# A vision-tower kernel on one core: one filter block's five-shift sum goes from VectorE to GpSimd, and two convolution products change places

## Chip, cores and metric

One core of one Trainium2 chip runs the whole program in one launch. The metric is the device time in microseconds (us); lower is better. All data is float32.

## What is computed

The reference takes 64 images of 84x84x3 and the weights of three blocks, and returns 64 x 25 tokens of 128 values:

```
xs = concat([x, shift_right(x), shift_left(x), shift_down(x), shift_up(x)])   # 15 channels
y  = conv2d(xs, conv_w, strides=(16, 16), "VALID") + conv_b                   # 25 tokens per image
y  = (y - mean(y)) * rsqrt(var(y) + 1e-3) * gamma + beta
h  = y @ dense_w + dense_b
h  = layernorm(h + attention(h))      # two softmax maps, their difference weighted by lambda, group norm
h  = layernorm(h + ffn(h))            # per-image FFN weights: W + sum over 8 experts of gate * tv_W
```

Only the first block, the tokenizer, is touched by the change. A shift of the image and a shift of the filter are the same thing, so the convolution over 15 channels can be done as one over the 3 image channels, with one filter that is the sum of the five shifted ones. The host lays out the five shifted copies of the filter (`conv_filter`, each on an 18x18x3 window, 972 rows of 128, padded to 1024, with the bias as one more row). The kernel sums them.

## The kernel before

**Tokenizer.** The 1024 rows of the filter are cut into KT = 8 blocks of 128 rows, which this text counts as k = 0 to 7; k = 6 is the seventh. The 1600 tokens are cut into steps of 256 for the loads and into units u = 0 to 3 for the work: three units of 512 tokens (two steps each) and one of 64. For each k:

- SyncE (`load_filter`, L398) loads the five copies of block k, 128 x 640 values, 320 KB, and adds 16 to `w_loaded[k]`.
- VectorE (`weff_sum(k)`) waits for that load, sums the five copies in one TENSOR_REDUCE (L787) into `wsum[:, k]`, waits for its own result, and sums each row of that to one number with a second TENSOR_REDUCE (L789, `rowsum`).
- ScalarE (`weff_centre(k)`, L560) waits for the row sum and writes rowsum - 128 * wsum, the centred filter block `weff[:, k]`, so that the layer norm's mean is zero without further work.
- TensorE (`conv(u, k)`, L1078) multiplies `weff[:, k]` with unit u's windows of block k, and adds over k into one PSUM bank for each unit. Each call stands in the trace as two weight loads and two MATMULs. Before an even k it waits for the windows of blocks k and k+1 of both steps (`load_windows`, L403: index j = k/2 and step s), and always for `weff_ready >= k + 1`.

VectorE runs `weff_sum(0)` to `weff_sum(7)` one after another as its first work, then `y_scale(0)`. ScalarE runs `weff_centre(0)` to `weff_centre(7)`, then `h_bias()` (L579), `y_square(0)` (L564), `y_rstd(0)` (L568, L570). All engines run in their written order, and a wait holds all that is behind it on that engine.

SyncE issues the loads in this order: filter 0; windows j=0, s=0,1; filter 1; windows j=0, s=2,3; filters 2, 3; windows j=1, s=0,1; filters 4, 5; windows j=2, s=0,1; filters 6, 7; windows j=3, s=0,1; the first constants (L418); windows of s=2,3 for j=1, 2, 3; the second constants (L421); windows of the last three steps; the last constants (L424).

**Order on TensorE.** It is written out by hand, from L1249 on. The part that matters:

```
conv(0, 0)  conv(1, 0)  conv(0, 1)  conv(1, 1)  conv(0, 2)  conv(0, 3)  conv(0, 4)  conv(0, 5)  conv(0, 6)
conv(1, 2)
conv(0, 7)
h_bias_product()          # L1084, 128x1; releases h_bias() on ScalarE
conv(1, 3)
y_var(0)                  # L1093, needs y_square(0)
conv(1, 4)  conv(1, 5)  conv(1, 6)  dense(0)  conv(1, 7)  proj(0, 0) ...
```

`conv(0, 7)` ends the sum of the first 512 tokens, and `y_square(0)` reads it. `conv(1, 2)` needs the windows j=1 of steps 2 and 3.

**GpSimd** begins with small memsets (L464 to L474), then waits for the first constants and makes `dgam` (L476, L478: gamma times the dense weights, needed by `dense(0)`), then for the second constants, makes small tiles from them (L482 to L491), clears `wrow` (L493, four memsets) and goes on with copies and softmax products. In the trace its first additions (TENSOR_TENSOR) come at L476.

**Later stages.** Projections (L1128), attention scores (L1172), value products (L1187), group norm, output projection, the gates, the merging of the per-image FFN weights (L1387, evacuated by VectorE at L382 and ScalarE at L381), their application (L1409, L1433), and the last two layer norms. `keep_long` (L1246) are products whose result nobody reads.

Of the kernel before, what the change touches and what calls it, by code (L numbers as in the profile page):

```python
# [29 lines left out]
KT = 8  # L30
NP = KT // 2
NSH = 5
# [55 lines left out]
UT = 2 * ST  # L88
Y_BANK = [2, 3, 2, 3]
VAR_BANK = 7  # L90
PROJ_BANK = [4, 5, 6, 4]
SLOT = [0, 0, 0, 0, 1, 0, 1, 0]


def unit_tokens(u):

    return min(UT, NTOK - u * UT)


def unit_steps(u):  # L100

    return range(2 * u, min(2 * u + 2, NSTEP))
# [10 lines left out]
def build(nc, cst_d, wconv_d, xcol_d, tvw_d, sce_d, scb_d, out_d):  # L113
    f32 = mybir.dt.float32
    bf16 = mybir.dt.bfloat16
    ALU = mybir.AluOpType
    ACT = mybir.ActivationFunctionType
    AX = mybir.AxisListType
    ctx = ExitStack()
    with ctx:  # L120
# [3 lines left out]
        def sem(name):  # L124
            return ctx.enter_context(nc.semaphore(name))
# [16 lines left out]
        def C(name, rows=P):  # L142
            a, b = COL[name]
            return cst[0:rows, a:b]
# [5 lines left out]
        w5 = hid[:, 0:KT * NSH * D]  # L150
        weff = hid[:, KT * NSH * D:KT * (NSH + 1) * D].rearrange("p (k d) -> p k d", k=KT)
        wsum = t6[:, 0:KT * D].rearrange("p (k d) -> p k d", k=KT)
        rowsum = sb("rowsum", KT)

        def windows(u, k):

            n = unit_tokens(u)
            a = arena[:, KT * UT * u:KT * UT * u + KT * n]
            if n < UT:
                return a.rearrange("p (k n) -> p k n", k=KT)[:, k]  # L160
            return a.rearrange("p (s k n) -> p s k n", s=2, k=KT)[:, :, k, :]

        def unit_cols(t, u):

            return t[:, UT * u:UT * u + unit_tokens(u)]
# [65 lines left out]
        w_loaded = [sem(f"w_loaded{i}") for i in range(KT)]  # L231
# [7 lines left out]
        rows_loaded = sem("rows_loaded")  # L239
        stored = sem("stored")  # L240
        wsum_done = sem("wsum_done")
        rowsum_done = sem("rowsum_done")
        weff_ready = sem("weff_ready")
        conv_done = sem("conv_done")
# [218 lines left out]
        def _(pool):  # L463
# [8 lines left out]
            for b in range(2):  # L472
                pool.memset(qT[b][:, NTOK:TP], 0.0).then_inc(pads_set, 1)
            pool.memset(t1[:, NTOK:].rearrange("p (b k) -> p b k", k=IB)[:, :, NS:IB], 0.0).then_inc(pads_set, 1)  # L474
            pool.wait_ge(first_loaded, 16)
            pool.tensor_tensor(dgam[:, :], C("dense_w"), C("gamma").to_broadcast([P, P]), ALU.mult).then_inc(dgam_ready, 1)  # L476
            pool.wait_ge(dgam_ready, 1)
# [65 lines left out]
            for s in range(NPS):  # L543
                pool.wait_ge(norm_done[2], 2 * (s + 1))
                c = slice(s * ST, (s + 1) * ST)
                v = t4[:, c].rearrange("p (t d) -> p t d", d=D)
# [6 lines left out]
        def _(act):  # L553
# [12 lines left out]
            def y_rstd(u):  # L566
                act.wait_ge(yvar_done, u + 1)
                act.activation(unit_cols(t5, u), PS[:, VAR_BANK, 0:unit_tokens(u)], ACT.Ln, bias=epsc[:, 0:1]).then_inc(yln_done, 1)  # L568
                act.wait_ge(yln_done, u + 1)
# [6 lines left out]
            def h_bias():  # L576
                act.wait_ge(first_loaded, 16)
                act.wait_ge(hb_done, 1)
                act.activation(hb[:, :], PS[:, VAR_BANK, 0:1], ACT.Identity, bias=C("dense_b")).then_inc(hb_ready, 1)  # L579

# [4 lines left out]
            def query_evac(c):  # L585
                act.wait_ge(proj_done[0], c + 1)
                act.activation(qT[0][:, c * QT:(c + 1) * QT], PS[:, PROJ_BANK[0], 0:QT], ACT.Copy).then_inc(proj_ready[0], 1)

            def keys_evac(c, b):
# [3 lines left out]
                act.wait_ge(proj_done[w], c + 1)  # L593
                src = PS[:, PROJ_BANK[w], 0:QT].rearrange("p (u k) -> p u k", u=2)
                for m in range(4):
# [185 lines left out]
        def _(dve):  # L781

            def weff_sum(k):

                dve.wait_ge(w_loaded[k], 16)
                v = w5.rearrange("p (k g d) -> p k d g", k=KT, g=NSH)[:, k]
                dve.tensor_reduce(wsum[:, k, :], v, AX.X, ALU.add).then_inc(wsum_done, 1)  # L787
                dve.wait_ge(wsum_done, k + 1)
                dve.tensor_reduce(rowsum[:, k:k + 1], wsum[:, k, :], AX.X, ALU.add).then_inc(rowsum_done, 1)  # L789

            def y_scale(u):
# [23 lines left out]
            def small_evac():  # L815
                dve.wait_ge(small_done, 1)
                dve.tensor_copy(cob[:, :], PS[:, VAR_BANK, 0:1]).then_inc(cob_ready, 1)
                dve.tensor_copy(lnaff[:, :], PS[:, VAR_BANK, 128:128 + 2 * D]).then_inc(lnaff_ready, 1)

            def key_evac(c):  # L820
                dve.wait_ge(kb_ready, 2)
                dve.wait_ge(proj_done[1], c + 1)
                src = PS[:, PROJ_BANK[1], 0:QT].rearrange("p (u k) -> p u k", u=2)
                for m in range(4):
# [3 lines left out]
            def key_raw():  # L828

                dve.wait_ge(second_loaded, 16)  # L830
                dve.wait_ge(proj_done[1], 2)
                src = PS[:, PROJ_BANK[1], 0:QT].rearrange("p (u k) -> p u k", u=2)
                dve.tensor_scalar(k1raw, src, C("k1_b"), None, ALU.add).then_inc(k1raw_ready, 1)

            def query_evac(b, c):
                w = 2 * b
                dve.wait_ge(proj_done[w], c + 1)
                dve.tensor_copy(qT[b][:, c * QT:(c + 1) * QT], PS[:, PROJ_BANK[w], 0:QT]).then_inc(proj_ready[w], 1)

# [73 lines left out]
            def gate_sum(q):  # L913
                dve.wait_ge(gh_ready, q + 1)
                dve.tensor_reduce(ghsum[:, q * QI:(q + 1) * QI], by_image(t5, q), AX.X, ALU.add).then_inc(ghsum_done, 1)

            weff_sum(0)
            weff_sum(1)
            weff_sum(2)
            weff_sum(3)  # L920
            weff_sum(4)
# [143 lines left out]
        def _(pe):  # L1065
            def conv(u, k):

                n = unit_tokens(u)
                if k % 2 == 0:
                    for s in unit_steps(u):  # L1070
                        pe.wait_ge(x_loaded[k // 2][s], 16)
                pe.wait_ge(weff_ready, k + 1)
                if k == 0 and u >= 2:
                    pe.wait_ge(h_ready, u - 1)
                dst = PS[:, Y_BANK[u], 0:n]
                if n == UT:
                    dst = dst.rearrange("p (s n) -> p s n", s=2)
                mm = pe.matmul(dst, weff[:, k, :], windows(u, k), start=(k == 0), stop=(k == KT - 1))  # L1078
                if k == KT - 1:
                    mm.then_inc(conv_done, 1)  # L1080

            def h_bias_product():
                pe.wait_ge(first_loaded, 16)
                pe.matmul(PS[:, VAR_BANK, 0:1], C("dense_w"), C("beta"), start=True, stop=True).then_inc(hb_done, 1)  # L1084

            def y_var(u):
# [4 lines left out]
                else:  # L1091
                    pe.wait_ge(yln_done, u)
                pe.matmul(PS[:, VAR_BANK, 0:unit_tokens(u)], yavg[:, :], unit_cols(t5, u), start=True, stop=True).then_inc(yvar_done, 1)  # L1093

# [19 lines left out]
            def proj(c, w):  # L1114
# [11 lines left out]
                if w == 3:  # L1126
                    pe.wait_ge(proj_ready[0], c + 1)
                pe.matmul(PS[:, PROJ_BANK[w], 0:QT], C(("q1", "k1", "q2", "k2")[w]), t2[:, c * QT:(c + 1) * QT], start=True, stop=True).then_inc(proj_done[w], 1)  # L1128

# [124 lines left out]
            conv(0, 4)  # L1254
            conv(0, 5)
            conv(0, 6)
            conv(1, 2)
            conv(0, 7)
            h_bias_product()
            conv(1, 3)  # L1260
            y_var(0)
# [318 lines left out]
```

## Time and profile before

| | us |
|---|---|
| median of 3 runs | 214.38 |
| lowest and highest of them | 212.93, 216.39 |
| the profiled execution | 213.37 |
| its span, first to last instruction | 211.6 |
| granted TensorE clock, mean over the span | 0.956 of full |

The profiled execution is a run of its own beside the three. Its span leaves out 213.37 - 211.6 = 1.8 us that lie around the instructions. Engines in the rows: PE is TensorE's matmuls, PEld its weight loads, DVE is VectorE, ACT ScalarE, POOL GpSimd, SPq the issue of a DMA by SyncE. Times of rows are counted from the span's start.

### The profile page before, as it was taken

The numbers are of one execution on the slowest core, as the hardware profiler recorded it, in microseconds if no ns is written. First come the engines' busy times: TensorE is split into PE (matmuls) and PEld (weight loads), VectorE is DVE, ScalarE is ACT, GpSimd is POOL, SyncE is SP. The second block draws the span as 40 slices with busy tenths as digits, with TensorE's granted clock in tenths as the row PEclk, the third lists the DMA queues.
The fourth block names the chain that finished last, engine by engine and source line by source line (L and its number), as shares of the span: only waits on it lengthen the run. The fifth ranks groups of instructions, "written<-read, shape, count | busy, mean of one in ns | idle before, by whom it ended". The sixth has DMA issues, their size and how long they took to land.

```text
span 211.6 us, 7823 instructions
## 1 busy us (share of the span) xinstructions
PE 176.7 (84%) x3432; PEld 121.3 (57%) x3432; DVE 134.4 (64%) x247; ACT 120.6 (57%) x223; POOL 55.5 (26%) x80
## 2 busy tenths in 40 slices
PE   0797999999999999898899999999999999980000
PEld 0233444466668765544788888888877777760000
DVE  2594146466999899784596666666664444489750
ACT  2131365387794523588475777777763333356991
POOL 2001681584278546000000000000070000037740
PEclk9999999999999999999999999999999999997555
DMA  6999994222200000000013121213000000000112
GB/s 203 384 392 386 375 300 110 83 84 64 59 6 3 5 3 3 6 0 0 3 31 86 55 64 46 71 37 81 5 5 3 3 3 3 3 3 0 39 47 69
DMA packets 9265, 16.51 MB, mean 78 GB/s; under 512 B 1598, under 2 KB 4350, under 8 KB 8720
## 3 DMA queue, kind: packets, MB, share of 16 engines
q1 hardware_dynamic: 9232, 16.02, 23.8%
q8 instruction: 27, 0.44, 0.9%
q14 instruction: 6, 0.05, 0.1%
HBM read 15.20 MB, written 0.82 MB: 76 GB/s over the span
## 4 chain that ended last, share of the span: by engine, by line
PE 62%; DVE 14%; ACT 11%; SPq 4%; DMA 4%; issue 3%; ACTq 0%
PE PS L1387 16%; DVE arena L382 8%; PE PS L1078 8%; PE PS L1409 7%; PE PS L1128 5%; ACT t L769 5%; PE PS L1246 4%; PE PS L1399 4%; PE PS L1172 4%; DMA arena<-windows 4%; PE PS L1187 3%; SPq L403 2%; PE PS L1146 2%; SPq L398 2%; PE PS L1098 2%
## 5 line engine op out<-in xcount | busy, mean ns | idle before, releaser
L382 DVE COPY arena<-PS 128x1024 f32<-128x1024 f32 x32 | 39.0, 1224 | 32.4 <-PE PS L1387 32.4
L381 ACT ACTIVATE arena<-PS 128x1024 f32<-128x1024 f32 x32 | 32.7, 1024 | 21.0 <-PE PS L1387 20.9
L1387 PE MATMUL PS<-gates,wrow 32*128 32x128 f32 x1024 | 37.2, 282 | 1.7 <-DVE arena L382 0.7
L1387 PEld LDWEIGHTS PS<-gates,wrow 32*128 32x128 f32 x1024 | 31.4, 186 | 7.8 <-DVE arena L382 5.3
L1078 PE MATMUL PS<-arena,hid 128*128 128x512 f32 (+1 forms) x64 | 27.3, 564 | 7.7 <-ACT hid L560 6.2
L1078 PEld LDWEIGHTS PS<-arena,hid 128*128 128x128 f32 x64 | 11.4, 205 | 21.7 <-issue 15.7
L539 POOL TENSOR_TENSOR t<-t,lnaff 128x2048 f32<-128x2048 f32 x1 | 4.6, 4568 | 71.2 <-PE PS L1399 71.2
L1433 PE MATMUL PS<-arena,hid 128*32 128x128 f32 x512 | 17.3, 276 | 0.0
L1409 PE MATMUL PS<-arena,t 128*32 128x128 f32 x512 | 17.3, 276 | 0.0
L769 ACT ACTIVATE t<-t,nms,rsl 128x128 f32<-128x128 f32 x32 | 13.4, 480 | 2.4 <-DVE nms L1048 2.4
L734 ACT ACTIVATE hid<-hid 128x400 f32<-128x400 f32 x16 | 8.5, 537 | 10.7 <-DVE hid L1005 10.7
L1433 PEld LDWEIGHTS PS<-arena,hid 128*32 128x32 f32 x512 | 13.0, 109 | 2.7 <-issue 2.7
L547 POOL TENSOR_TENSOR t<-t,lnaff 128x256 f32<-128x256 f32 x8 | 5.8, 726 | 32.6 <-ACT t L769 32.6
L1409 PEld LDWEIGHTS PS<-arena,t 128*32 128x32 f32 x512 | 13.0, 109 | 1.9
L787 DVE TENSOR_REDUCE t<-hid 128x128 f32<-128x640 f32 x8 | 9.9, 1244 | 6.1 <-DMA hid<-conv_filter 6.1
L1128 PE MATMUL PS<-t,cst 128*128 128x400 f32 x32 | 12.6, 512 | 0.3 <-ACT hid L596 0.3
L521 POOL TENSOR_TENSOR arena<-arena,wr 128x800 f32<-128x800 f32 x8 | 12.3, 1538 | 0.6
L560 ACT ACTIVATE hid<-t,rowsum 128x128 f32<-128x128 f32 x8 | 3.2, 402 | 13.5 <-DVE rowsum L789 13.5
L1399 PE MATMUL PS<-cst,t 128*128 128x128 f32 x64 | 10.5, 286 | 0.4 <-ACT t L727 0.4
L596 ACT ACTIVATE hid<-PS,kb,headmask 128x400 f32<-128x400 f32 x16 | 9.7, 688 | 0.5 <-PE PS L1128 0.3
L1246 PE MATMUL PS<-t,cst 128*128 128x512 f32 x20 | 9.9, 608 | 0.0
L727 ACT ACTIVATE t<-PS 128x512 f32<-128x512 f32 x16 | 9.3, 581 | 1.0 <-PE PS L1409 1.0
(133 smaller groups left out, 302.5 us busy)
## 6 DMA issues: line engine op xcount, KB each, us to landing
arena<-windows SPq DMA_DIRECT2D x24, 256.0 KB, 8.2
wrow<-ffn_weights SPq DMA_DIRECT2D x32, 128.0 KB
hid<-conv_filter SPq DMA_DIRECT2D x8, 320.0 KB, 6.3
wrow<-ffn_weights SPq DMA_DIRECT2D x64, 8.0 KB
cst<-consts SPq DMA_DIRECT2D x1, 840.0 KB, 11.6
out<-t SPq DMA_DIRECT2D x16, 50.0 KB
cst<-consts SPq DMA_DIRECT2D x1, 322.0 KB, 9.3
arena<-windows SPq DMA_DIRECT2D x4, 64.0 KB, 8.7
```

What stands on the lines that cost most here:

```text
L381: return eng.activation(dst, PS[:, b:b + 2, :], ACT.Copy)
L382: return eng.tensor_copy(dst, PS[:, b:b + 2, :])
L521: pool.tensor_tensor(ev, ev, wr[:, c].unsqueeze(2).to_broadcast([P, UX, NS]), ALU.mult).then_inc(scaled, 1)
L769: act.activation(dst[:, c], t4[:, c], ACT.Identity, bias=nms[:, k:k + 1], scale=rsl[:, k:k + 1]).then_inc(norm_done[L], 1)
L787: dve.tensor_reduce(wsum[:, k, :], v, AX.X, ALU.add).then_inc(wsum_done, 1)
L1078: mm = pe.matmul(dst, weff[:, k, :], windows(u, k), start=(k == 0), stop=(k == KT - 1))
L1128: pe.matmul(PS[:, PROJ_BANK[w], 0:QT], C(("q1", "k1", "q2", "k2")[w]), t2[:, c * QT:(c + 1) * QT], start=True, stop=True).then_inc(proj_do ...
L1246: pe.matmul(PS[:, bank, :], ident, t2[:, 0:512], start=True, stop=True)
L1387: mm = pe.matmul(PS[:, merge_bank(n) + r, :].rearrange("p (b k j) -> p k b j", k=4, j=NJ)[:, k], wrow[32 * r:32 * r + 32, w], gates[32 * r ...
L1399: mm = pe.transpose(PS[:, 6 + i % 2, g * P:(g + 1) * P], t1[:, c:c + P], ident)
L1409: mm = pe.matmul(PS[32 * (b % 4):32 * (b % 4) + 32, 4 + i % 2, (b // 4) * P:(b // 4 + 1) * P], t3[:, im * IB:(im + 1) * IB], wm[c % 2][:, ...
L1433: mm = pe.matmul(PS[32 * (b % 4):32 * (b % 4) + 32, 4 + q, (b // 4) * D:(b // 4 + 1) * D], hidv[:, c, im * NS:im * NS + 32], wm[c % 2][:, ...
```

## The change

Two edits. GpSimd, ahead of its wait for the first constants, waits for filter block KG = 6 and makes its five-shift sum by four additions, each of which waits for the one before; VectorE's `weff_sum(6)` no longer does the first TENSOR_REDUCE but waits for the fourth addition, and then makes the row sum as before. And on TensorE `conv(0, 7)` stands ahead of `conv(1, 2)` instead of behind it.

```
+KG = 6
...
+        wpart_done = sem("wpart_done")
...
             pool.memset(t1[:, NTOK:].rearrange("p (b k) -> p b k", k=IB)[:, :, NS:IB], 0.0).then_inc(pads_set, 1)
+            v = w5.rearrange("p (k g d) -> p k g d", k=KT, g=NSH)[:, KG]
+            pool.wait_ge(w_loaded[KG], 16)
+            pool.tensor_tensor(wsum[:, KG, :], v[:, 0], v[:, 1], ALU.add).then_inc(wpart_done, 1)
+            for g in range(2, NSH):
+                pool.wait_ge(wpart_done, g - 1)
+                pool.tensor_tensor(wsum[:, KG, :], wsum[:, KG, :], v[:, g], ALU.add).then_inc(wpart_done, 1)
             pool.wait_ge(first_loaded, 16)
...
             def weff_sum(k):
-                dve.wait_ge(w_loaded[k], 16)
-                v = w5.rearrange("p (k g d) -> p k d g", k=KT, g=NSH)[:, k]
-                dve.tensor_reduce(wsum[:, k, :], v, AX.X, ALU.add).then_inc(wsum_done, 1)
-                dve.wait_ge(wsum_done, k + 1)
+                if k == KG:
+                    dve.wait_ge(wpart_done, NSH - 1)
+                else:
+                    dve.wait_ge(w_loaded[k], 16)
+                    v = w5.rearrange("p (k g d) -> p k d g", k=KT, g=NSH)[:, k]
+                    dve.tensor_reduce(wsum[:, k, :], v, AX.X, ALU.add).then_inc(wsum_done, 1)
+                    dve.wait_ge(wsum_done, k + 1 if k < KG else k)
                 dve.tensor_reduce(rowsum[:, k:k + 1], wsum[:, k, :], AX.X, ALU.add).then_inc(rowsum_done, 1)
...
             conv(0, 6)
+            conv(0, 7)
             conv(1, 2)
-            conv(0, 7)
             h_bias_product()
```

## Rows read from the trace of the kernel before

**Rows 1.** The page: busy us of each engine, share of the span, instructions.

```profile
PE 176.7 (84%) x3432; PEld 121.3 (57%) x3432; DVE 134.4 (64%) x247; ACT 120.6 (57%) x223; POOL 55.5 (26%) x80
```

**Rows 2.** The chain that ended last, 0 to 80 us: start, us, what.

```profile
9.49 8.02 DMA arena<-windows
...
19.13 1.95 PE PS L1078 x4
...
52.75 2.42 ACT hid L596 x4
```

**Rows 3.** Timeline, TensorE's weight loads: start, us; in brackets idle before, and releaser.

```profile
17.57 0.30 PEld L1078 LDWEIGHTS PS<-arena,hid 128*128 128x128 f32 x2 [1.45 <-DMA arena<-windows]
19.10 0.30 PEld L1078 LDWEIGHTS PS<-arena,hid 128*128 128x128 f32 x2 [1.23 <-DMA arena<-windows]
...
22.10 0.30 PEld L1093 LDWEIGHTS PS<-t,yavg 128*128 128x128 f32 x2 [0.77 <-ACT t L564]
```

**Rows 4.** Timeline of VectorE, 15 to 17 us.

```profile
15.05 0.29 DVE L789 TENSOR_REDUCE rowsum<-t 128x1 f32<-128x128 f32 x1
15.28 1.25 DVE L787 TENSOR_REDUCE t<-hid 128x128 f32<-128x640 f32 x1
16.56 0.29 DVE L789 TENSOR_REDUCE rowsum<-t 128x1 f32<-128x128 f32 x1
16.77 1.24 DVE L787 TENSOR_REDUCE t<-hid 128x128 f32<-128x640 f32 x1
```

**Rows 5.** Timeline of ScalarE, 16 to 22 us.

```profile
16.88 0.40 ACT L560 ACTIVATE hid<-t,rowsum 128x128 f32<-128x128 f32 x1 [1.11 <-DVE rowsum L789]
18.36 0.40 ACT L560 ACTIVATE hid<-t,rowsum 128x128 f32<-128x128 f32 x1 [1.07 <-DVE rowsum L789]
21.30 0.26 ACT L579 ACTIVATE hb<-PS,cst 128x1 f32<-128x1 f32 x1 [2.54 <-PE PS L1084]
21.46 0.59 ACT L564 ACTIVATE t<-PS 128x512 f32<-128x512 f32 x1
```

**Rows 6.** Loads of filter blocks 6 and 7, issued at 7.92 and 8.52 us.

```profile
L398 SPq DMA_DIRECT2D hid<-conv_filter x2: 434/493/552, 7.9 to 8.5; - x2
DMA to landing us min/median/max: 7.3/7.5/7.6
```

**Rows 7.** Window loads j=1 of steps 2 and 3, issued at 10.44 and 10.87.

```profile
DMA to landing us min/median/max: 7.9/8.0/8.1
```

**Rows 8.** GpSimd's groups by shape: count, busy us, mean ns, idle before.

```profile
L547 POOL TENSOR_TENSOR t<-t,lnaff 128x256 f32<-128x256 f32 x8 | 5.8, 726 | 32.6 <-ACT t L769 32.6
L539 POOL TENSOR_TENSOR t<-t,lnaff 128x2048 f32<-128x2048 f32 x1 | 4.6, 4568 | 71.2 <-PE PS L1399 71.2
L518 POOL TENSOR_TENSOR wr<-rec,lamw 128x32 f32<-128x32 f32 x8 | 2.0, 252 | 14.0 <-DVE rec L863 13.9
L476 POOL TENSOR_TENSOR dgam<-cst 128x128 f32<-128x128 f32 x1 | 0.4, 399 | 15.9 <-DMA cst<-consts 15.9
```

**Rows 9.** Timeline of GpSimd, 2 to 23 us.

```profile
17.77 0.40 POOL L476 TENSOR_TENSOR dgam<-cst 128x128 f32<-128x128 f32 x1 [15.89 <-DMA cst<-consts]
18.26 0.55 POOL L478 TENSOR_SCALAR dgam<-dgam 128x128 f32<-128x128 f32 x1
22.64 0.20 POOL L482 TENSOR_TENSOR rowhalf<-cst 128x2 f32<-128x2 f32 x1 [3.84 <-DMA cst<-consts]
```

**Rows 10.** Stretches: us, busy time of each engine, granted clock (PEclk), DMA share, GB/s.

```profile
12.05:19.00 6.95, 5.82 (x13) 1.88 (x11) 6.14 (x9) 2.01 (x5) 0.95 (x2) 1.00 1.05 386
188.00:193.00 5.00, 1.60 (x42) 1.10 (x34) 4.15 (x21) 3.29 (x11) 3.85 (x6) 0.99 0.00 0
```

**Rows 11.** Timeline: TensorE's weight loads around 12 us, and its last products.

```profile
11.20 0.34 PEld L1078 LDWEIGHTS PS<-arena,hid 128*128 128x128 f32 x1 [0.52 <-issue]
12.05 0.19 PEld L1078 LDWEIGHTS PS<-arena,hid 128*128 128x128 f32 x1 [0.52 <-issue]
12.48 0.19 PEld L1078 LDWEIGHTS PS<-arena,hid 128*128 128x128 f32 x1 [0.24 <-issue]
...
188.52 1.08 PE L1433 MATMUL PS<-arena,hid 128*32 128x128 f32 x32
```

## Prediction, made before the changed kernel ran

> **What bounds the kernel.** I read four views, in this order. The page first: TensorE is busy for 176.7 of 211.6 us, far more than any other engine [rows 1]. Then the chain that ended last, cut to the stretch around the change. It runs over window loads until 17.51 us, then over TensorE; from 19.13 us it is TensorE's own work, piece after piece, until ScalarE takes over for one step at 52.75 [rows 2]. So what moves the moment at which TensorE sets off at 19.13 should move everything behind it by as much. Third, the timeline of each engine between 13 and 25 us, to see who releases whom. Fourth, the GpSimd rows that resemble the new additions.
>
> The timelines give this order of events before. Filter block 6 is issued at 7.92 and lands 7.3 later [rows 6], at 15.2; VectorE starts to sum it at 15.28, 0.06 before the previous row sum is over [rows 4], so the load and VectorE are ready together. The sum takes 1.25, the row sum starts at 16.56, block 7 follows at 16.77 [rows 4]. ScalarE centres block 6 from 16.88 to 17.28 and block 7 from 18.36 to 18.76 [rows 5]. TensorE does conv(0, 6) at 17.57, released not by the filter (ready at 17.28) but by the windows that land at 9.49 + 8.02 = 17.51 [rows 2, 3]. Then conv(1, 2) at 19.10, released by its windows, issued at 10.87 and landed 8.1 later, at about 19.0 [rows 3, 7]. The pair conv(1, 2), conv(0, 7) takes 1.95, to 21.08 [rows 2], and released by the bias product behind it ScalarE does the bias at 21.30 and the square at 21.46 [rows 5].
>
> **The change, part by part.**
>
> *Removed:* one TENSOR_REDUCE of 1.25 us on VectorE. In the written order that alone would bring block 7 forward by up to 1.25, to 17.51.
>
> *Added:* four additions of 128x128 on GpSimd. They need block 6 in full, so they can't start before about 15.28, the moment at which VectorE started on it. GpSimd is idle then: its memsets are done and its next work starts at 17.77 [rows 9]. Duration of one: the nearest row is the 128x128 product with a broadcast operand, 0.399 [rows 8]; between the 128x32 (0.252) and the 128x256 (0.726) a straight line gives 0.252 + 96/224 x 0.474 = 0.455 [rows 8]. I take 0.43, between the two. The step between dependent instructions is 0.09 (18.17 to 18.26) [rows 9]. So 4 x 0.43 + 3 x 0.09 = 1.99, and the sum is ready at 17.27. That is 0.7 later than VectorE had it (16.53). Bounds: with 0.252 each 1.28, ready at 16.56; with 0.726 each 3.17, ready at 18.45.
>
> The Trainium skill, GPSIMD Engine Reference, section Engine selection, gives reductions along the free dimension to VectorE; its section on elementwise accounting has about 2.6 cycles per element and 4497 ns for 2048 columns. The trace agrees with the long case: 4.57 us for 128x2048 [rows 8]. An estimate from that page's figures for 128 columns is 128 x 2.6 / 1.2 GHz = 0.28 plus 0.06 of fixed cost, 0.34, which gives a sum at 16.91 and would leave the total within 0.1 us of before; the 128x128 row here is 0.399, so the row decides.
>
> *The wait that is added:* VectorE's row sum 6 now waits for GpSimd, and queued behind it is the sum of block 7, whose filter landed about 0.9 after block 6 (8.52 + 7.6 = 16.1) [rows 6]. VectorE runs in written order, so it idles from 15.34. Row sum 6 starts at 17.31 instead of 16.56 (0.04 for the release). ScalarE follows 0.32 later (16.56 to 16.88) and takes 0.40: block 6 is ready at 18.03. Conv(0, 6) goes from 17.57 to 18.07; the filter is now what comes last, not the windows. Sum 7 starts 0.21 after row sum 6 (16.56 to 16.77), at 17.52, and block 7 is ready 1.99 after that (16.77 to 18.76): 19.51, against 18.76 before [rows 4, 5].
>
> *The exchange on TensorE:* conv(0, 7) now stands first. It starts at 19.51 + 0.04 = 19.55 in place of conv(1, 2) at 19.10. Conv(1, 2) has had its windows since 19.0 but is queued behind. With the old order conv(1, 2) would still start at 19.10, end its issue 0.86 later at 19.96, and conv(0, 7) would find its filter ready since 19.51: the late block would cost nothing. So the exchange uncovers what GpSimd added. Alone, without GpSimd's part, it would gain: conv(0, 7) at 18.80, the pair over 0.3 earlier. Together the pair starts 19.55 - 19.10 = 0.45 later.
>
> *Behind it:* the bias product comes after both in either order, and ScalarE's square waits behind the bias, so the square of the first tokens doesn't profit from an earlier conv(0, 7); it comes 0.45 later as well. The product that needs it waits for it already (22.10, released by L564) [rows 3]. Everything on the chain follows by 0.45.
>
> *On GpSimd:* the additions are over at 17.27, before the first constants let dgam start at 17.77, so dgam isn't moved; if they took 0.726 each it would start 0.65 late, and its reader, dense(0), needs y_scale(0), which comes behind the square at 21.46 [rows 5]. What follows waits for the second constants at 22.64 anyway [rows 9]. SyncE's queue is untouched. The added instructions cost nothing beyond this.
>
> **Sum.** 213.37 + 0.45 = 213.8 us, against the profiled execution. That execution lies 1.0 below the median of the three runs shown; by the median the same sum gives 214.8. I forecast 213.8, slightly slower, a difference below what can be told (2%, 4.3 us, is about what a measurement of this kernel can tell from no change). With the additions from 0.38 to 0.50 each it is +0.2 to +0.7 us.
>
> **Rivals.**
>
> 1. *It works as drawn: a gain.* If the sum of block 6 is there by 16.56, VectorE loses nothing. With the sum then, block 7 comes at 18.76 as before, the exchange starts the pair at 18.80 instead of 19.10: -0.3, 213.1. If it were there at 15.3, as if the sum were free, block 7 would be ready at 17.5, conv(0, 7) would follow conv(0, 6) directly at 18.46, and the gain would be 0.65: 212.7. For it: VectorE is busy nearly all the time from 10.7 on, and in an execution in which filter 6 lands 0.7 earlier GpSimd would work beside VectorE's sum of block 5. Against it: here the load lands as VectorE gets free, so nothing is left to overlap; and four additions at the price of a 128x32 one are needed.
>
> 2. *The additions are dearer.* At 0.726 each the sum is ready at 18.45, block 7 at 18.49 + 0.21 + 1.99 = 20.69, and the pair starts 1.6 late: 215.0. It decides from 0.5 us each. For it: they are the first additions that GpSimd does, and a plain operand costs more than a broadcast one may. Against it: the 0.399 of L476 is itself a first addition.
>
> 3. *TensorE's clock falls (slower).* The hole before conv(0, 6) grows by 0.50 and the one behind it stays. If the granted clock went from 2.4 to 1.2 GHz there, products would be spaced 0.85 instead of 0.43 us per record (11.20 to 12.05 against 12.05 to 12.48) [rows 11]. An estimate: at that spacing the four records of the pair take 4 x 0.42 = 1.7 us more, the ten from conv(0, 6) to y_var(0) 4.2. With the 0.45 that is 215.5 if the clock is back after the pair, and 218.0 if it isn't before y_var(0) is done, 4.6 over the profiled run and past the limit of 2%. Decided by whether the holes of 1.1 and 0.5 us are enough. Against it: over 12.05 to 19.00 the clock is 1.00 with 5.82 of 6.95 busy, and at the end TensorE is idle from 189.6, and the mean clock of 188 to 193 is still 0.99 [rows 10, 11]. The Trainium skill, TensorE: Matmul & The Clock Gate, section What's actually happening, says that the clock falls back when TensorE has been idle for a while; the trace's end agrees, and its longest new hole is much shorter than those 3.4 us.
>
> 4. *It is drowned.* The change shows nowhere, because a later wait takes up 0.4 us: 213.4. For it: the chain leaves TensorE at 52.75 and crosses VectorE and ScalarE many times later. Against it: those all wait for products of the same chain, and no load with a fixed time ends late on it.
>
> **Chances.** Forecast (+0.2 to +0.7) 0.58; rival 1 0.15; rival 2 0.17; rival 3 0.03; rival 4 0.07. The range must hold the scatter of runs, 212.93 to 216.39, as a median dampens it: 212.6 to 215.8. From below it covers a gain of 0.7, from above the costliest additions and a median like the one shown. Over 2% faster has no case that reaches it: 0.01. Over 2% slower needs the clock: 0.02. Within 2%: 0.97.
>
> **What would show each step.** In the profile after: four TENSOR_TENSOR rows of 0.40 to 0.46 on GpSimd from about 15.28 on, the last over near 17.3; VectorE idle from 15.34 to 17.3, released by GpSimd; ScalarE's seventh and eighth L560 at about 17.6 and 19.1; conv(0, 6) released by ScalarE at 18.0 rather than by a DMA; conv(0, 7) released by ScalarE near 19.5; the bias at 21.7 instead of 21.30; granted clock 1.00 over 12 to 26 us. The forecast is wrong if conv(0, 7) starts before 19.1, if the additions last over 0.5 each, or if the shift of 0.4 at 21 us is not there any more at 50 and at 180 us.

## The result, and the profile after

The changed kernel took 214.23 us (median of 20 runs, 213.17 to 216.29), the kernel before 213.24 in 20 runs of its own (212.46 to 216.39). The ratio is 1.0050, 95% interval 1.0032 to 1.0069: slower by some 1.1 us, within 2% as forecast, but more than twice the forecast 0.45. The ratios leave out single executions that lie over 1.5% above the fastest of their kernel. The direction came out as forecast, and so did the path on which the delay travels; its size did not. The time of 213.8 was forecast from a profiled execution; the measured median lies 0.4 above it, inside the stated range. In the profiled executions the span went from 211.6 to 212.4.

The chain that ended last, in the changed kernel (start, us, what):

```profile
7.78 7.75 DMA hid<-conv_filter
15.52 0.07 issue
15.59 0.47 POOL t L479
...
17.19 0.46 POOL t L482
17.66 0.02 issue
17.68 0.28 DVE rowsum L800
17.96 1.17 DVE t L798
...
19.16 0.30 DVE rowsum L800
19.45 0.02 issue
19.48 0.41 ACT hid L568
19.89 0.04 issue
19.93 1.98 PE PS L1089 x4
21.92 0.12 PE PS L1095 x2
...
53.58 2.42 ACT hid L604 x4
```

Line numbers moved by 2 to 11: L1089 is conv (L1078 before), L568 the centring (L560), L800 and L798 VectorE's two reductions (L789, L787), L604 was L596 and L1444 was L1433. Before, the chain came to TensorE by a load of windows [rows 2]. Now it comes by the load of filter block 6, GpSimd's four additions, the row sum, the sum of block 7 that was queued behind it, its row sum and ScalarE; the conv(0, 7) that sets off at 19.93 is the first of the pair, as this text calls conv(0, 7) and conv(1, 2) together. From there on nothing changed: from the pair's start to ScalarE's step at 53.58 are 33.65 us, and 52.75 - 19.10 = 33.65 before [rows 2, 3]. The shift of 0.83 us is still there in the last products of the feed-forward part, in the chains of the kernel before and of the changed one:

```profile
184.18 1.05 PE PS L1433 x32
185.01 1.05 PE PS L1444 x32
```

The three engines, from their timelines; first GpSimd:

```profile
15.59 0.46 POOL L479 TENSOR_TENSOR t<-hid 128x128 f32<-128x128 f32 x1 [13.71 <-DMA hid<-conv_filter]
16.13 1.52 POOL L482 TENSOR_TENSOR t<-t,hid 128x128 f32<-128x128 f32 x3
18.02 0.40 POOL L484 TENSOR_TENSOR dgam<-cst 128x128 f32<-128x128 f32 x1 [0.37 <-DMA cst<-consts]
```

VectorE (compare [rows 4]):

```profile
15.28 0.28 DVE L800 TENSOR_REDUCE rowsum<-t 128x1 f32<-128x128 f32 x1
17.68 0.28 DVE L800 TENSOR_REDUCE rowsum<-t 128x1 f32<-128x128 f32 x1 [2.12 <-POOL t L482]
17.88 1.24 DVE L798 TENSOR_REDUCE t<-hid 128x128 f32<-128x640 f32 x1
```

TensorE's weight loads (compare [rows 3]):

```profile
16.05 0.30 PEld L1089 LDWEIGHTS PS<-arena,hid 128*128 128x128 f32 x2 [1.00 <-ACT hid L568]
18.51 0.30 PEld L1089 LDWEIGHTS PS<-arena,hid 128*128 128x128 f32 x2 [2.17 <-issue]
19.93 0.30 PEld L1089 LDWEIGHTS PS<-arena,hid 128*128 128x128 f32 x2 [1.12 <-ACT hid L568]
```

VectorE, idle for 2.12 us although block 7 had landed at 16.34, is the added wait; the pair at 19.93, released by ScalarE and not by windows, is the exchange. All loads of this execution landed a little late: filter block 6 at 15.52 against 15.26. The edit's own cost is therefore read from the landing of block 6 on: 3.84 us to the pair before (19.10 - 15.26), 4.41 after (19.93 - 15.52). That is +0.57 us. The rest of the 0.83 between the two pair starts is the loads' own scatter. This way of counting is sound because the loads keep their distances: block 6 landed anywhere from 14.88 to 15.74 in the 14 traces of this text, but block 7 always landed 0.82 to 0.85 behind it, and the windows that release the pair in the kernel before 3.76 to 3.80 behind it. So the 3.84 of the one trace of the kernel before is not a chance of that trace. The distance from landing to pair is what the experiments are compared by below.

### The profile page after: what moved, and what is told of

It reads as the page before. It is cut to its first block, busy times and chain, and to the rows that moved or that the text cites. A ratio compares the mean times of both kernels' runs of the same rounds, so it can differ in the third digit from the quotient of the medians.

```text
span 212.4 us, 7826 instructions
## 1 busy us (share of the span) xinstructions
PE 176.2 (83%) x3432; PEld 121.1 (57%) x3432; DVE 133.3 (63%) x246; ACT 120.6 (57%) x223; POOL 57.3 (27%) x84
## 4 chain that ended last, share of the span: by engine, by line
PE 61%; DVE 14%; ACT 11%; DMA 4%; SPq 3%; issue 3%; POOL 1%; ACTq 0%
PE PS L1398 16%; DVE arena L384 8%; PE PS L1420 7%; PE PS L1089 7%; PE PS L1139 5%; ACT t L777 5%; PE PS L1257 4%; PE PS L1410 4%; PE PS L1183 4%; DMA hid<-conv_filter 4%; PE PS L1198 3%; PE PS L1157 2%; SPq L405 2%; PE PS L1109 2%; PE PS L1104 1%
## 5 line engine op out<-in xcount | busy, mean ns | idle before, releaser
L1089 PE MATMUL PS<-arena,hid 128*128 128x512 f32 (+1 forms) x64 | 26.8, 554 | 9.0 <-DMA arena<-windows 7.1
L1089 PEld LDWEIGHTS PS<-arena,hid 128*128 128x128 f32 x64 | 11.1, 202 | 22.8 <-issue 16.3
L1444 PE MATMUL PS<-arena,hid 128*32 128x128 f32 x512 | 17.3, 276 | 0.0
L1444 PEld LDWEIGHTS PS<-arena,hid 128*32 128x32 f32 x512 | 13.0, 110 | 2.7 <-issue 2.7
L798 DVE TENSOR_REDUCE t<-hid 128x128 f32<-128x640 f32 x7 | 8.7, 1243 | 6.3 <-DMA hid<-conv_filter 6.3
L568 ACT ACTIVATE hid<-t,rowsum 128x128 f32<-128x128 f32 x8 | 3.2, 402 | 14.6 <-DVE rowsum L800 14.6
L604 ACT ACTIVATE hid<-PS,kb,headmask 128x400 f32<-128x400 f32 x16 | 9.7, 688 | 0.4 <-PE PS L1139 0.3
```

The source lines that it names most:

```text
L604: act.activation(keys(b, c)[:, :, m, :], src, ACT.Identity, bias=kb[:, 4 * b + m:4 * b + m + 1], scale=headmask[:, m:m + 1]).then_inc(proj ...
L1444: mm = pe.matmul(PS[32 * (b % 4):32 * (b % 4) + 32, 4 + q, (b // 4) * D:(b // 4 + 1) * D], hidv[:, c, im * NS:im * NS + 32], wm[c % 2][:, ...
```

## The experiments

Theory 1: the pair starts when block 7's filter is ready, that is a fixed time after block 6 lands, and everything behind moves by as much. Rivals: GpSimd's part costs by itself (theory 2), by contention, by VectorE's wait, or by a hole that takes TensorE's clock; or a late pair costs more than its lateness (theory 3). "Landing to pair" is from the trace of each run; "to ScalarE" is from the pair to the step that stands at 52.75 in [rows 2]. With block 7 first the pair follows conv(0, 6) without a gap, and its start is taken as 0.86 behind that of conv(0, 6); the sum of the two distances doesn't depend on that. The first ratio of the changed kernel, 1.0050, is in the section above; each group was measured against its own runs of the kernel before (medians 212.85, 213.02, 213.20), on two chips.

| kernel | landing to pair | to ScalarE | ratio | 95% interval |
|---|---|---|---|---|
| before | 3.84 | 33.65 | 1 | |
| changed, again | 4.41 | 33.65 | 1.0053 | 1.0024 to 1.0083 |
| exchange alone | 3.56 | 33.65 | 0.9978 | 0.9950 to 1.0007 |
| GpSimd alone | 3.82 | 33.68 | 1.0005 | 0.9978 to 1.0033 |
| block 7 first | 3.87 | 33.64 | 1.0015 | 0.9987 to 1.0042 |
| hole filled | 4.42 | 33.65 | 1.0042 | 1.0014 to 1.0070 |
| block 5 | 3.70 | 33.65 | 0.9998 | 0.9973 to 1.0023 |
| square first | 3.56 | 33.45 | 0.9988 | 0.9967 to 1.0010 |
| sum twice | 6.53 | 35.69 | 1.0244 | 1.0207 to 1.0280 |
| twice, filled | 6.55 | 33.65 | 1.0109 | 1.0069 to 1.0148 |

The intervals reach some 0.3% to either side, as much as most of the effects. By the ratios alone the changed kernel differs from the one before, from the exchange alone, from block 5 and from the square first, and the sum done twice differs from all others; what else is said of single rows rests on the traces.

**The exchange alone.** VectorE sums all blocks.

```
             conv(0, 6)
+            conv(0, 7)
             conv(1, 2)
-            conv(0, 7)
             h_bias_product()
```

> The kernel before with the exchange on TensorE alone; VectorE sums all eight blocks. Theory 1 (the pair conv(0, 7), conv(1, 2) starts when block 7 is ready, and all behind it moves by as much): block 7 ready at 18.76, conv(0, 7) at 18.80 in place of a pair start at 19.10, -0.3 us, ratio 0.9985, and the pair's start moves with VectorE's sum, not with the windows. Theory 2 (the exchange itself costs, because conv(1, 2) no longer fills the hole and TensorE's clock suffers in some executions): a wider spread of times, ratio 1.002 or more, some executions with a lower granted clock.

The pair came 0.28 earlier, as expected, released by ScalarE. Weight loads on TensorE:

```profile
17.22 0.30 PEld L1078 LDWEIGHTS PS<-arena,hid 128*128 128x128 f32 x2 [1.44 <-DMA arena<-windows]
18.48 0.30 PEld L1078 LDWEIGHTS PS<-arena,hid 128*128 128x128 f32 x2 [0.95 <-ACT hid L560]
```

and on ScalarE:

```profile
18.02 0.40 ACT L560 ACTIVATE hid<-t,rowsum 128x128 f32<-128x128 f32 x1 [1.07 <-DVE rowsum L789]
```

The chain of this trace names a load of windows as the pair's releaser. The times speak for ScalarE: the pair starts 0.46 after ScalarE's last centring did, as in the changed kernel (19.48 to 19.93), and the windows that conv(1, 2) needs landed only at 18.68, 0.20 after conv(0, 7) had started.

The ratio of 0.9978 agrees with 0.9985 and excludes the 1.002 of theory 2; that it is a gain can't be told from the ratio (its interval holds 1), only from the trace.

**GpSimd's part alone.** The changed kernel with the old order.

```
             conv(0, 6)
-            conv(0, 7)
             conv(1, 2)
+            conv(0, 7)
             h_bias_product()
```

> The changed kernel with the old order on TensorE: conv(1, 2) ahead of conv(0, 7), GpSimd sums block 6. Theory 1: GpSimd's sum makes block 7 ready about 0.8 to 0.9 later than before, near 19.6 for a landing of block 6 at 15.26; conv(1, 2) starts with its windows at 19.10, conv(0, 7) at 19.96 and finds its filter: 0.0 to +0.1 us, ratio 1.000. Theory 2 (GpSimd's part costs by itself, for instance by the longer hole ahead of conv(0, 6)): ratio 1.003 or more.

```profile
18.38 0.30 PEld L1089 LDWEIGHTS PS<-arena,hid 128*128 128x128 f32 x2 [2.14 <-issue]
19.21 0.33 PEld L1089 LDWEIGHTS PS<-arena,hid 128*128 128x128 f32 x2 [0.53 <-issue]
19.80 0.19 PEld L1089 LDWEIGHTS PS<-arena,hid 128*128 128x128 f32 x1 [0.26 <-ACT hid L568]
```

In these weight loads conv(0, 6) is late (18.38, 2.99 after the landing at 15.39, against 2.31 before), conv(1, 2) follows at 19.21, 3.82 after the landing, where it stood before (its windows had landed at 19.15), and conv(0, 7) at 19.80 is released by ScalarE without holding TensorE up: its first MATMUL runs on behind conv(1, 2) without idle time. The late block is covered. The ratio of 1.0005 fits, but its interval reaches the 1.003 of theory 2; it is the trace that shows no delay. So neither part loses by itself. The exchange gains 0.28, GpSimd's part loses nothing, and both together lose 0.57: the exchange takes away what hid the late block.

**Block 7 ahead of the wait.** What is queued behind the added wait is done before it.

```
             weff_sum(5)
+            dve.wait_ge(w_loaded[7], 16)
+            v = w5.rearrange("p (k g d) -> p k d g", k=KT, g=NSH)[:, 7]
+            dve.tensor_reduce(wsum[:, 7, :], v, AX.X, ALU.add).then_inc(wsum_done, 1)
             weff_sum(6)
-            weff_sum(7)
+            dve.wait_ge(wsum_done, 7)
+            dve.tensor_reduce(rowsum[:, 7:8], wsum[:, 7, :], AX.X, ALU.add).then_inc(rowsum_done, 1)
```

> The changed kernel, but VectorE sums block 7 before it waits for GpSimd, and then makes row sums 6 and 7. This takes away what is queued behind the added wait. Theory 1: row sum 6 still at about 17.5 after the landing at 15.26, row sum 7 0.2 later, block 6 ready at 18.2, block 7 at 18.6; conv(0, 6) at 18.25, conv(0, 7) right behind it at 19.1: no later than before, -0.1 to +0.1 us, ratio 1.000 (0.9955 against the changed kernel). Theory 2 (the late conv(0, 6) and the hole ahead of it cost the clock): the hole stays, so ratio 1.003 or more and the spread of the changed kernel.

VectorE's timeline:

```profile
15.75 1.25 DVE L936 TENSOR_REDUCE t<-hid 128x128 f32<-128x640 f32 x1 [0.78 <-DMA hid<-conv_filter]
17.06 0.29 DVE L800 TENSOR_REDUCE rowsum<-t 128x1 f32<-128x128 f32 x1
17.26 0.28 DVE L939 TENSOR_REDUCE rowsum<-t 128x1 f32<-128x128 f32 x1
```

Here both engines work at once, and neither is slowed: VectorE's sum takes 1.25 as ever, GpSimd's last three additions 1.53 against 1.52. So contention between the two is no part of the cost. Conv(0, 6) is as late as in the changed kernel (3.01 after the landing), but conv(0, 7) follows it directly, and the pair is back at 3.87; ScalarE's step comes 37.51 after the landing, against 37.49 before and 38.06 in the changed kernel. So against the kernel before, the whole 0.57 was the block queued behind the wait. The wait itself is not free: against the exchange alone (3.56) 0.31 is left, because conv(0, 6) is late.

**The hole filled.** Products that nobody reads.

```
             conv(0, 5)
+            for _ in range(2):
+                pe.matmul(PS[:, VAR_BANK, 0:P], weff[:, 5, :], windows(0, 5)[:, 0, 0:P], start=True, stop=True)
+            pe.matmul(PS[:, VAR_BANK, :].rearrange("p (s n) -> p s n", s=2), weff[:, 5, :], windows(0, 5), start=True, stop=True)
             conv(0, 6)
```

> The changed kernel with 1.3 us of products that nobody reads (into the unused bank 7) in the hole between conv(0, 5) and conv(0, 6); nothing else changed. Theory 1: nothing changes, conv(0, 6) is released by ScalarE all the same: +0.6 to +0.9 us against before, ratio 1.003 to 1.005 as for the changed kernel. Theory 2 (in some executions the hole costs granted clock): the excess over the profile's 0.6 goes, ratio 1.003 or less, and the slow half of the changed kernel's runs (over 214.5) disappears.

Landing to pair 4.42, and the ratio 1.0042: nothing gained that can be seen, so the hole of the changed kernel (1.37 us with TensorE idle) isn't what costs. The interval alone (from 1.0014) would leave theory 2 open; against it speak the traces, which have the full clock over the hole both filled and empty. Two of the 12 runs were still over 215.

**The changed kernel again.** Unaltered.

> The changed kernel once more, unaltered, so that its ratio stands beside those of its neighbours on one chip. The profiles put the start of the pair 0.57 us later than before, counted from the landing of block 6 (4.41 against 3.84). Theory 1 (that is all there is): +0.6 us, ratio 1.0027; the 1.005 of the first measurement was high by scatter. Theory 3 (the late pair costs more than the profiled executions show, in the others): 1.004 to 1.005 again.

1.0053, close to the 1.0050 of the first measurement, though the medians of these runs (213.67 and 213.02) are only 0.65 us apart, 1.0031. The 1.0027 that the profiles' 0.57 us amount to lies inside the second interval (from 1.0024) and outside the first (from 1.0032). The next runs ask where the rest is.

**Block 5 instead of block 6.** One constant: KG = 5.

> The changed kernel with GpSimd summing block 5 instead of block 6. Block 5 lands 2.18 us ahead of block 6, so GpSimd's 2.1 us end as block 6 lands and nearly nothing waits. Theory 1: row sum 5 just before the landing of block 6, sum 6 0.2 after it, block 7 ready 3.67 after it, the pair at 3.72 against 3.84 before and 4.41 in the changed kernel: -0.1 us, ratio 0.9995. Theory 2 (any sum on GpSimd costs here, by VectorE's wait or by contention for memory): ratio 1.002 or more, or VectorE's sums longer than 1.25 us.

VectorE again:

```profile
14.86 0.29 DVE L800 TENSOR_REDUCE rowsum<-t 128x1 f32<-128x128 f32 x1 [1.40 <-POOL t L482]
15.07 1.24 DVE L798 TENSOR_REDUCE t<-hid 128x128 f32<-128x640 f32 x1
```

GpSimd's sum ended as block 6 landed (14.88 in this run), and the wait of 1.40 us on VectorE cost only 0.14 against the exchange alone. But it didn't gain either, although block 5 had landed at 12.70, 0.77 before VectorE was free for it (13.47). The same edit on the block before it, with the exchange, is level with the kernel before (0.9998).

**The square first.** The exchange alone, and on ScalarE:

```
-            h_bias()
             y_square(0)
+            h_bias()
             y_rstd(0)
```

> The exchange alone (VectorE sums all blocks) and, on ScalarE, the first square ahead of the bias. With the exchange alone the square waited for the bias product, which stands behind conv(1, 2). Theory 1: the square starts when conv(0, 7) is done, about 1.3 us earlier, and the product that reads it no longer waits; only the hole of about 0.2 us ahead of that product is to be had: -0.3 from the exchange and -0.2 from this, ratio 0.9975. Rival (the chain is TensorE's own work and that hole is not real): as the exchange alone, 0.9985.

On ScalarE:

```profile
19.78 0.60 ACT L564 ACTIVATE t<-PS 128x512 f32<-128x512 f32 x1 [1.22 <-PE PS L1078]
```

The square started at 19.78, 1.16 after the pair against 2.36 with the exchange alone, and the distance to ScalarE fell from 33.65 to 33.45: the 0.2 us are real in the trace. The ratio of 0.9988 doesn't show them beside the exchange alone (0.9978); the intervals overlap, and neither version can be told from the kernel before by its time.

**The sum done twice.** A dose: four more additions ahead of the four, into `dgam`, which gets its own values only later.

```
-            pool.tensor_tensor(wsum[:, KG, :], v[:, 0], v[:, 1], ALU.add).then_inc(wpart_done, 1)
-            for g in range(2, NSH):
-                pool.wait_ge(wpart_done, g - 1)
-                pool.tensor_tensor(wsum[:, KG, :], wsum[:, KG, :], v[:, g], ALU.add).then_inc(wpart_done, 1)
+            for i, acc in enumerate((dgam[:, :], wsum[:, KG, :])):
+                if i:
+                    pool.wait_ge(wpart_done, NSH - 1)
+                pool.tensor_tensor(acc, v[:, 0], v[:, 1], ALU.add).then_inc(wpart_done, 1)
+                for g in range(2, NSH):
+                    pool.wait_ge(wpart_done, i * (NSH - 1) + g - 1)
+                    pool.tensor_tensor(acc, acc, v[:, g], ALU.add).then_inc(wpart_done, 1)
...
-                    dve.wait_ge(wpart_done, NSH - 1)
+                    dve.wait_ge(wpart_done, 2 * (NSH - 1))
```

> The changed kernel with the four additions done twice on GpSimd, the first time into a scratch tile; VectorE waits for the eighth. Theory 1 (the wait is on the chain, one for one): four more additions of 0.535 us from start to start, 2.14 us, move the pair, the whole chain and the time by 2.1 us: pair 6.55 after the landing of block 6, ratio 1.0127 against before. Theory 3 (each us of lateness costs more than a us): over 1.015. Rival (a later wait takes part of it up): under 1.010.

The pair came at 6.53, as computed, but the ratio was 1.0244, 5.2 us for 2.7. The stretches of this run's trace (us, busy time by engine, PEclk, DMA share, GB/s) say why:

```profile
12.00:18.60 6.60, 4.59 (x11) 1.42 (x9) 3.10 (x5) 1.20 (x3) 2.96 (x7) 1.00 1.05 391
18.65:25.45 6.80, 5.21 (x6) 2.13 (x7) 1.73 (x3) 0.80 (x2) 4.24 (x11) 0.50 1.06 381
25.45:32.00 6.55, 6.55 (x17) 2.61 (x15) 0.69 (x1) 2.75 (x5) 5.36 (x4) 1.00 1.07 307
```

and its TensorE timeline:

```profile
15.65 1.12 PE L1092 MATMUL PS<-arena,hid 128*128 128x512 f32 x2 [0.19 <-ACT hid L571]
20.24 5.41 PE L1092 MATMUL PS<-arena,hid 128*128 128x512 f32 x6 [3.46 <-ACT hid L571]
```

TensorE was idle for 3.46 us, its granted clock fell from 2.4 to 1.2 GHz at 18.65, and conv(0, 6) and the pair ran at that level; from the pair to ScalarE's step it needed 2.04 us more than the changed kernel. With the pair's own 2.69 (6.53 - 3.84) that makes 4.73 of the 5.2. This is the clock rival of the prediction, at twice the dose.

**Twice, with the hole filled.** The same, with four products of 512 columns ahead of conv(0, 6):

```
             conv(0, 5)
+            for _ in range(4):
+                pe.matmul(PS[:, VAR_BANK, :].rearrange("p (s n) -> p s n", s=2), weff[:, 5, :], windows(0, 5), start=True, stop=True)
             conv(0, 6)
```

> The kernel with the sum done twice, and in the hole between conv(0, 5) and conv(0, 6) four products of 512 columns that nobody reads, 3.4 us at the full clock. With the sum twice and the hole empty the granted clock was 0.5 from 18.65 to 25.48 and the ratio 1.0244. Clock theory (the long hole takes TensorE's clock, and that is what made the cost two for one): the clock stays 1.00, the pair starts 6.55 after the landing of block 6, +2.7 us, ratio 1.0127 to 1.014. Rival (the cost comes from the lateness itself, by stages behind): 1.022 or more as before, with the clock at 1.00.

```profile
18.65:25.45 6.80, 6.46 (x16) 2.39 (x15) 1.74 (x3) 1.55 (x4) 4.25 (x12) 1.00 1.05 381
```

The clock of the same stretch is 1.00, and the ratio falls to 1.0109, by some 2.9 us (0.0135 of 213, each of the two against its own runs of the kernel before), with 3.4 us of work added and the pair no earlier. So one us of lateness costs about one us, as long as TensorE is kept busy: 2.71 us would be 1.0127, inside the interval. The second us was the clock. Theory 3 falls for the lateness, and stands for a hole of 3.5 us.

**Three more traces of the changed kernel.** To see whether its own hole of 1.4 us costs the clock in executions other than the profiled one.

> The changed kernel, one look, for another execution's clock record. Of 32 executions of it 12 had a mean granted clock of 0.952 or less and most of these were some 1.4 us longer than the rest; of the kernel before 16 of 64. If such an execution is met, the record says where the low stretch lies. Theory (the hole ahead of conv(0, 6)): from about 16 to 20 us on. Rival (a chance of the whole program): elsewhere.

> As the look before it: the changed kernel, another execution. A mean clock of 0.955 to 0.960 means no low stretch inside, and a time near 213.5; 0.944 to 0.951 one inside, 1.4 us or more longer.

> As the two looks before it: the changed kernel, a third execution, with the same two possible pictures.

All three have the pair at 4.40 or 4.41 after the landing and the full clock over the hole. The second and third executions took 213.32 and 213.75 with mean clocks of 0.956 and 0.955. The first took 214.69 with 0.951, and has a low stretch, but not there. Its stretches:

```profile
86.00:89.40 3.40, 2.98 (x135) 2.24 (x134) 2.31 (x7) 2.27 (x6) 0.00 (x0) 1.00 0.00 0
89.40:92.80 3.40, 3.40 (x11) 2.26 (x10) 3.02 (x8) 1.72 (x5) 0.00 (x0) 0.50 0.02 5
92.80:96.20 3.40, 2.92 (x12) 1.60 (x11) 1.98 (x4) 2.47 (x8) 0.00 (x0) 0.99 0.00 0
```

and of the second trace the first of the same stretches:

```profile
86.00:89.40 3.40, 2.78 (x135) 2.24 (x134) 2.12 (x7) 2.10 (x5) 0.00 (x0) 1.00 0.02 5
```

That is the end of the attention, behind 128 short products of 32x50, 70 us behind the change. The second execution had the same work at that place and kept the full clock, so what decides is open. From the step at 53.27 to the start of the last group of products of the feed-forward part this execution needed 132.24 us, the second 131.35, the third 131.16: 0.9 to 1.1 us more. A second such stretch stands in the trace of the sum done twice with the hole filled: from 91.6 to 95.05 its granted clock was 0.51, at the same place of a program that runs some 2 us later. These two traces are also the ones with a mean clock of 0.951; the eleven that have no low stretch between 14 us and their last product have 0.955 to 0.960. So the rival was right in both: the low stretch lies far from the edit, in a part that the edit doesn't touch.

## Why the prediction was right or wrong

**The path.** Right in its order of events: additions in series from the landing of block 6 on, VectorE idle behind them, conv(0, 6) released by ScalarE instead of by windows (18.51, forecast 18.07), conv(0, 7) released by ScalarE (19.93, forecast 19.55), the square behind the bias, and the shift carried without loss: 33.65 us from the pair to ScalarE's step in both, and 131.43 from there to the start of the last group of products in both. dgam wasn't moved by the additions; it started at 18.02, 0.07 after its constants landed.

**The exchange uncovers it.** Right, and shown by three runs: the exchange alone 3.56, GpSimd alone 3.82, both 4.41, where the prediction had -0.3, 0 and +0.45 against the 3.84 of before.

**The price of the sum: mis-sized.** The step that failed is "I take 0.43, between the two", and with it the start. An addition took 0.46 to 0.47, above the 0.455 of the straight line through the 128x32 and 128x256 rows; the pull towards the 0.399 of L476, whose second operand is a broadcast, was wrong; whether the broadcast is what made that row shorter, no run shows. From start to start it was 0.535, so the four took 2.07 (15.59 to 17.66) instead of 1.99. The first addition started 0.07 after the landing, where 0.02 was assumed from VectorE's start. 0.08 + 0.05 = 0.13, which is the step from 0.45 to 0.57 within the rounding of the rows. The estimate of 0.34 from the Trainium skill (GPSIMD Engine Reference, the section on elementwise accounting) was further off still: the trace shows 0.46. The straight line through the rows has 0.18 us that don't depend on the number of columns, an estimate from 0.252 for 32 and 0.726 for 256, where the prediction's estimate had 0.06.

**The other half of the 1.1 us: no term for it.** The mis-sized price explains 0.12 of the 0.6 us between forecast and measurement. For the rest the prediction had nothing: "The added instructions cost nothing beyond this", it says, and it priced one execution without a term for how executions differ. The profiles show 0.57. In the second comparison the executions with a mean granted clock above 0.952 had medians of 213.50 (8 runs) and 212.88 (22 runs of the kernel before), which is 0.62 and agrees. The others, some 1.1 to 1.5 us longer in the median, were 4 of 12 in the changed kernel and 5 of 27 before. Over all groups with a clock record they were 13 of 35 against 18 of 75, so a larger share of them may account for 0.13 x 1.3 = 0.17 us, an estimate. Whether that share differs by more than chance is open. Nor does the mean clock tell all: one execution of the changed kernel took 215.12 with 0.959, and block 6 landed from 14.93 to 15.74 in its five traces, while the kernel before has only one trace to compare. So which step failed for this half stays open. What the runs do show is where it was not found: not in the hole ahead of conv(0, 6) (full clock over it in five traces, and 1.0042 with it filled), and not between the pair and the last products (the same 33.65 and 131.43 us in the profiled executions of both).

**Slips in its working.** *Removed* and the first rival have block 7 ready at 17.5 if GpSimd's sum were free. But block 7 lands only at 16.10, so by the prediction's own steps it could be ready at 16.10 + 0.02 + 1.99 = 18.11 at best, 0.65 earlier than before and not 1.25; conv(0, 7) would still have followed conv(0, 6) directly. The hole ahead of conv(0, 6) grew from 0.65 to 1.37, by 0.72 and not 0.50, and the one behind it shrank from 0.43 to 0.29. With additions of 0.726, dgam would come 18.45 - 17.77 = 0.68 late, not 0.65. And a difference of 0.5% was not below what can be told: 20 executions of each kernel gave an interval that excludes 1.

**The rivals.** A gain from GpSimd at work beside VectorE needs block 6 to land well before VectorE is free. In every trace with VectorE at work on block 5 it landed 0.04 to 0.10 us before, and as all loads move together an earlier execution changes nothing in that. Moving the edit one block forward gave the kernel before its time back. Dearer additions: right in direction, by a tenth of the distance. The clock: right as a mechanism and rightly given little chance here, since 1.23 to 1.37 us idle didn't do it in five traces of the changed kernel; a hole of 3.46 did. But one argument against it was weak. It took the end of the trace, idle for 3.4 us at a mean clock of 0.99, as a measure of what a hole may last. In the kernel with the sum done twice the clock fell 1.9 us after TensorE had gone idle. Drowned: no, the shift of 0.83 us is there at 53 and at 185 us.

## What to carry to other kernels

A sum moved to an idle engine can help only if its input is there before the first engine gets free, and by more than the idle engine is slower: here four additions took 2.14 us from the landing to their end and VectorE's one instruction 1.27 from its landing, so some 0.9 us ahead, an estimate. Block 5, 0.77 ahead, was not enough, and no run here shows such a gain. Where a load arrives just as that engine is ready, the slower engine simply stands in the path, and a wait in written order holds back the next block as well. Put ready work ahead of such a wait, as the third experiment did; it got the 0.57 us back. Two edits that are each harmless can lose together: work that stood first and was ready in time may have been hiding something late.

## What the runs showed of the hardware

The granted TensorE clock fell from 2.4 to 1.2 GHz 1.9 us after TensorE had gone idle (16.77 to 18.65) in the kernel with the sum done twice, and stayed low until 25.48 though the engine was at work again from 20.24; with 1.23 to 1.37 us idle it did not fall. The time from going idle to the fall is not one number: behind the last product of the program it was 2.5 to 4.5 us in the 14 traces (3.3 in the kernel before, 4.5 in the changed one). Filling the long hole with unread products was worth some 2.9 us. And a short low stretch can come with no hole in sight, behind many small products, in some executions and not in others (89.4 to 92.8 us in one of the five traces of the changed kernel, 91.6 to 95.05 in one of its variants), for about 1 us, so a difference of half a per cent is to be looked for in the clock's record before it is looked for in the edit. The DMA loads of this program landed up to 0.9 us apart from one execution to another (block 6 from 14.88 to 15.74), but together: the distances between them repeated within 0.05 us.
